# One-hots for two chunks from one two-operand comparison, in a four-layer graph network kernel

## What is computed

```python
x = layernorm(x + gat(x, ...))                  # layer 0
# layer 1: rows of a table summed by destination
h   = x @ W
out = segment_sum(h[src] * norm[:, None], dst, N)
x = layernorm(x + out)
# layer 2: twice, with edge weights
h   = x @ W1
out = segment_sum((dinv[row] * w * dinv[col])[:, None] * h[row], col, n) + b
x = layernorm(x + relu(...))                    # second time with W2
x = layernorm(x + layer3(x))                    # layer 3: same sums, the other direction
```

## Time and profile before

| | us |
|---|---|
| median of 3 runs (lowest, highest) | 3349.37 (3339.74, 3351.67) |
| the profiled execution: its own time | 3360.17 |
| its span, first to last instruction | 3358.4 |
| pass 1 (gathers) | 230.7 to 1413.3 |
| pass 2 (gathers) | 1430.7 to 2108.1 |
| pass 3 (gathers) | 2109.4 to 2794.2 |
| last layer, no gathers | from 2804 |

### The profile page before, as it was taken

The page is one execution under the profiler, slowest core; times in us unless marked ns, Lnnn a source line. Parts: engine busy times, 40 slices in busy tenths (PEclk is TensorE's granted clock), DMA queues, the critical chain, the costliest instruction groups (busy, mean ns, idle before and its releaser), DMA issues.

```text
span 3358.4 us, 58810 instructions
## 1 busy us (share of the span) xinstructions
PE 3159.1 (94%) x18605; PEld 2556.9 (76%) x18605; DVE 2313.6 (69%) x9060; ACT 1722.8 (51%) x4557; POOL 2046.4 (61%) x2015
## 2 busy tenths in 40 slices
PE   6789999999999999899999999799999998999999
PEld 5666777767767767678878888688888886888887
DVE  5657998998999889667777777466666664323323
ACT  3554767767767767534444444344444443232232
POOL 6627777777777777677777777577777772000000
PEclk9889999999999999999999999899999999999999
DMA  6256878778878778666666666676666666444443
GB/s 198 76 178 190 252 239 251 249 235 255 253 237 258 245 228 257 213 200 198 204 195 203 203 200 203 226 216 212 213 213 211 213 201 230 149 140 154 166 166 116
DMA packets 335272, 692.21 MB, mean 206 GB/s; under 512 B 63028, under 2 KB 180496, under 8 KB 334062
## 3 DMA queue, kind: packets, MB, share of 16 engines
q1 hardware_dynamic: 237134, 424.16, 37.4%
q0 software_dynamic: 95888, 262.38, 27.9%
q10 hardware_dynamic: 1936, 1.84, 0.2%
HBM read 497.33 MB, written 190.82 MB: 205 GB/s over the span
## 4 chain that ended last, share of the span: by engine, by line
PE 68%; DVE 12%; DMA 10%; POOL 4%; ACT 3%; issue 3%; SPq 0%; ACTq 0%; DVEq 0%
PE PS L1927 22%; PE PS L1999 15%; DMA G<-T,idx 7%; PE PS L1968 7%; PE PS L1970 6%; PE PS L1891 3%; POOL G L2062 2%; PE PS L1757 2%; PE PS L1867 2%; PE PS L1758 2%; DVE soh L1375 2%; PE PS L1858 2%; PE PS L1879 2%; PE PS L1908 1%; DVE M L1266 1%
## 5 line engine op out<-in xcount | busy, mean ns | idle before, releaser
L2062 POOL DMA_INDIRECT G<-T,idx x1890 | 1925.8, 1019 | 647.5 <-issue 275.4
L1927 PE MATMUL PS<-H,aw 128*128 128x256 f32 x4116 | 1052.0, 381 | 0.4 <-DMA aw<-AW 0.4
L1612 ACT ACTIVATE R<-G,wD 128x256 fp32r<-128x256 f32 x1008 | 508.8, 508 | 714.5 <-PE PS L1970 443.3
L1927 PEld LDWEIGHTS PS<-H,aw 128*128 128x128 f32 x4116 | 770.9, 191 | 110.5 <-DMA aw<-AW 0.8
L1275 DVE SCALAR_TENSOR_TENSOR R<-G,wD,R 128x256 fp32r<-128x256 f32 x1008 | 490.1, 486 | 389.4 <-ACT R L1612 385.2
L1968 PE MATMUL PS<-G,M 128*128 128x257 f32 x1764 | 572.5, 408 | 82.3 <-DMA G<-T,idx 32.5
L1970 PE MATMUL PS<-R,Mr 128*128 128x512 f32 x1008 | 583.6, 580 | 31.3 <-DVE R L1275 29.2
L1999 PE MATMUL PS<-HH,cr 128*128 128x512 f32 x2205 | 501.5, 389 | 0.3 <-DVE cr L1453 0.2
L1999 PEld LDWEIGHTS PS<-HH,cr 128*128 128x128 f32 x2205 | 413.3, 188 | 88.3 <-DVE cr L1453 2.6
L1655 ACT CAST atp<-PS 128x512 bf16<-128x512 f32 x588 | 336.5, 572 | 180.8 <-PE PS L1879 174.7
L1968 PEld LDWEIGHTS PS<-G,M 128*128 128x128 f32 x1764 | 297.9, 198 | 160.1 <-DVE M L1266 22.1
(11 more groups left out here) (231 smaller groups left out, 3908.5 us busy)
## 6 DMA issues: line engine op xcount, KB each, us to landing
aw<-AW SPq DMA_DIRECT2D x294, 448.0 KB
AT<-atp SPq DMA_DIRECT2D x539, 128.0 KB
br<-AT SPq DMA_DIRECT2D x77, 896.0 KB, 4.9
AW<-awp SPq DMA_DIRECT2D x264, 256.0 KB
G<-T,idx POOLq DMA_INDIRECT x1890
AT<-atf SPq DMA_DIRECT2D x49, 256.0 KB
T<-H SPq DMA_DIRECT2D x96, 128.0 KB
cr<-AT SPq DMA_DIRECT2D x7, 1024.0 KB, 4.8
```

The lines of the kernel that those rows point to most:

```text
L1612: e.activation(R[m % NR][:, 0:D], G[slot][:, 0:D], ACT.Copy, scale=wD[:, k // NC, k % NC:k % NC + 1]).then_inc(s_rw, 1)
L1927: ins = e.matmul(ps, aw[n_ % NAW][:, s_ % 7, :], H[:, s_, :], start=s_ == 0, stop=s_ == NBK - 1)
L2062: e.indirect_dma_start(G[slot][:, 0:D], None, TAB[p][0:N, :], bass.IndirectOffsetOnAxis(ap=idx[:, k // NC, k % NC:k % NC + 1], axis=0)).th ...
```

## The change

- `onehot` acts on even m only, and writes the one-hots of chunks m and m + 1 at once into a tile of 128 x 128 x 2: element (j, i) is 1 where `dlo` of chunk m + i is j. The two one-hots lie interleaved, element by element. It is a `tensor_tensor` whose two inputs are `iot2` (the ramp with each number twice, 256 columns) and two columns of `dlo`, repeated.
- NM is 3 tiles of two chunks; the pair m, m + 1 waits for the matmul of chunk m - 5.
- PE takes its stationary operand from the tile with a step of two elements (8 bytes). In pass 1 a matmul waits for the pair's instruction.
- `iot2` is written once, early, by a copy.

```diff
-NG, NM, NX = 7, 4, 4
+NG, NM, NX = 7, 3, 4
...
-        M = [tiles(onehots)(f"M{i}", [P, P]) for i in range(NM)]
+        M = [tiles(onehots)(f"M{i}", [P, P, 2]) for i in range(NM)]
         onehots.close()
-        Mr = [sb(f"Mr{i}", [P, P], F32R) for i in range(NM)]
+        Mr = [sb(f"Mr{i}", [P, P, 2], F32R) for i in range(NM)]
+        iot2 = sb("iot2", [P, P, 2])
...
+            done(e.tensor_copy(iot2[:, :, :], iot[:, :].unsqueeze(2).to_broadcast([P, P, 2])), "iot2")
...
             def onehot(p, k):
                 m = MOFF[p] + k
                 b, c = k // NC, k % NC
-                w.wait_ge(s_mm, m - NM + 1)
-                if p == 1:
-                    ins = e.tensor_scalar(M[m % NM][:, :], iot[:, :], dlo[:, b, c:c + 1], None, ALU.is_equal)
-                else:
-                    ins = e.tensor_scalar(Mr[m % NM][:, :], iot[:, :], dlo[:, b, c:c + 1], None, ALU.is_equal)
-                done(ins, ("M", m))
+                if m % 2 == 0:
+                    w.wait_ge(s_mm, m - 2 * NM + 2)
+                    done(e.tensor_tensor((M if p == 1 else Mr)[m // 2 % NM][:, :, :], iot2[:, :, :],
+                                         dlo[:, b, c:c + 2].unsqueeze(1).to_broadcast([P, P, 2]), ALU.is_equal), ("M", m))
...
-                    w.wait_ge(s_v, at["M", m] if p == 1 else at["low", m])
+                    w.wait_ge(s_v, at["M", m - m % 2] if p == 1 else at["low", m])
...
-                        e.matmul(ps, M[m % NM][:, :], G[slot][:, 0:D + 1], start=c == 0, stop=c == NC - 1).then_inc(s_mm, 1)
+                        e.matmul(ps, M[m // 2 % NM][:, :, m % 2], G[slot][:, 0:D + 1], start=c == 0, stop=c == NC - 1).then_inc(s_mm, 1)
                     else:
-                        e.matmul(ps, Mr[m % NM][:, :], R[m % NR][:, :], start=c == 0, stop=c == NC - 1).then_inc(s_mm, 1)
+                        e.matmul(ps, Mr[m // 2 % NM][:, :, m % 2], R[m % NR][:, :], start=c == 0, stop=c == NC - 1).then_inc(s_mm, 1)
...
-    nc = bacc.Bacc("TRN2", target_bir_lowering=False, num_devices=1)
+    nc = bacc.Bacc("TRN2", target_bir_lowering=False, num_devices=1, dynamic_dma_scratch_size=4096)
```

More of the change, by code:

```diff
@@ L1429, in aggregate @@
                     w.wait_ge(s_wn, 6)
+                after("iot2")
                 onehot(p, 0)
```

## The result

The changed kernel takes **3364.91 us** (median of 7 runs, 3356.97 to 3375.29) where the kernel before, timed beside it, takes 3347.86 (median of 7, 3339.74 to 3351.67). The ratio is 1.0057, 95% interval 1.0041 to 1.0073: slower by 14 to 24 us, 19 by the ratio, 17 by the medians. One warning on what follows: in two of the four later groups of runs the kernel before itself took 3838 and 3786 us, and those runs are compared only with the runs of before in their own group.

What follows compares the result with a forecast made beforehand. POOL's gathers were taken to bound passes 1 and 2, PE's dense units pass 3. Delays of 18.5 + 10.6 + 0 less 5.8 back gave +23.3 us on 3349.4: 3372.7 us, range 3338 to 3405 (8 in 10).

Steps and rivals of the forecast that it cites:

- POOL bounds passes 1 and 2: Gathers plus 0.305 us steps fill pass 1 (1173 of 1184 us) and pass 2 (679 of 679).
- The price of 42 ns: Gather delay per new two-input comparison, ends 0 and 90: 18.5 us in pass 1, 10.6 in pass 2.
- The counts of passes 2 and 3: Pass 2 taken as 504 gathers, 252 pairs; pass 3 as 505 gathers with 34 us to spare.
- What the removed one-hots cost POOL: Gathers starting beside old one-input one-hots, 0.02 us each: 5.8 us back, ends 0 and 12.
- By pass: Pass 1 longer by 12 to 20 us, pass 2 priced at 10.6, pass 3 unchanged.
- DVE's time at nothing: DVE relieved of 38 us over 945 pairs, hidden by POOL in passes 1 and 2 and PE in pass 3.
- Weights at a step at nothing: PE's weight loads at a step of 8 bytes were priced at 0 us.
- Loads over 200 ns: Sign set to prove the forecast wrong: PE's weight loads of L1970 or L1968 taking over 200 ns.
- The wait and the descriptor space at nothing: DVE's pair waiting for matmul m - 5, and the smaller gather descriptor space: 0 us each.
- The one-hots held POOL up: Rival, 12%: the old one-hots delayed gathers in passes 1 and 2, so the change is faster, 3315 us.
- Hardly delays: Rival, 25%: new comparisons delay gathers only 10 ns each, adding 7 us with 5.8 back: no change, 3350.5 us.
- Slow weights: Rival, 5%: 1008 weight loads in passes 2 and 3 each show 0.1 us, adding 100 us: 3473 us.

Runs made afterwards that it cites:

- scratch_only: The kernel before with only the smaller space for gather descriptors (4096): 3348.29 us, ratio 0.9990 to before.
- step_only: The changed kernel, but each one-hot written by its own one-input comparison into every second element of the shared tile: 3352.68 us, ratio 1.0000 to before.
- flat_tiles: The changed kernel with the pair's two one-hots one behind the other, so weights lie without a step: 3369.82 us, ratio 1.0059 to before.
- pass1_only: The changed kernel with the two-input comparison in pass 1 alone, one-input comparisons in passes 2 and 3: 3360.01 us, ratio 1.0028 to before.
- extra_two_again: The changed kernel plus 482 two-input comparisons in passes 1 and 2, into a tile nobody reads: 3431.29 us, ratio 1.0243 to before.
- extra_one_again: The changed kernel plus 482 one-input comparisons of the same output in passes 1 and 2, into an unread tile: 3390.80 us, ratio 1.0121 to before.

## Why the prediction came out as it did

The forecast was 3372.7 us, the measured median is 3364.9, inside the range of 3338 to 3405 (the forecast stood on 3349.4 for before, which the seven runs put at 3347.9); slower by over 0.5%, given 49%, is where the ratio of 1.0057 lies, though its interval reaches down across that bound.

- **POOL bounds passes 1 and 2: right.** In every kernel that was slower while before took some 3350 us, the gathers of the two passes are longer. Against the 1435.5 us of scratch_only and step_only they grew by 15 us in flat_tiles and 14 in pass1_only, whose medians lie 18 and 8 us above before, with DVE and PE less busy or as busy as before; in extra_two_again and extra_one_again they grew by 92 and 49 us, and the medians by 77 and 36. PE's wait for gathers rose as said.
- **The price of 42 ns: right on the mean, by luck in part.** The table gives 29.8 us over 441 + 261 = 702 new comparisons of passes 1 and 2: 42 ns. But it is 21.9 us over 441 in pass 1, 50 ns, and 7.9 over 261 in pass 2, 30 ns; one price for both passes was too low in one and too high in the other, and the two errors cancel. It is a price for these places only. Put right in front of another two-input comparison the same instruction costs 120; the end of 90 was too low for that, since it left out how joins close.
- **The counts of passes 2 and 3: a slip.** The window's edge was taken for the end of pass 2. It has 261 pairs, not 252, worth 0.4 us. POOL's bound there stands: 541.4 + 522 x 0.305 = 701 of 702.3 us. Pass 3 has 486 gathers, and before 479.8 us of them: 479.8 + 486 x 0.305 = 628 of 642.9 us. That leaves 15 us to spare, not 34, which still covers the 10.6 priced there.
- **"What the removed one-hots cost POOL", 5.8 us with ends 0 and 12: the term that was mis-sized.** The table puts it at 7.8 to 10.7 us, 9.2 on the mean. The prediction priced each at 0.02 us, with one place shown, where nothing was delayed, though a third of those gathers (52 of 152 in before) take 1 us or more: 23 are let in at the end of the one-hot itself and 27 at the end of a two-input instruction behind it. With 9.2 the sum is 29.5 - 9.2 = 20.3 us; with 5.8 it was 23.3. Both lie inside the interval of 14 to 24, so the times alone do not tell them apart.
- **A term that the prediction did not have.** Gathers that start outside the one-hots are held up some 5 us less with pairs than without (the account under the table). Why was not tested. It is of the size of what the sum is still too high by (20.3 against the measured 17 to 19) and somewhat larger.
- **By pass: half right.** Pass 1 was to grow by 12 to 20 us; pass1_only says 9.4, the profile pair 7.6, and three traces against three some 10. Pass 2 then brings 8 to 10 by the times and 6 by the traces, where 10.6 and a share of the 5.8 back were forecast. The profile pair shows nothing in pass 2, because before's profile had an unusually long one there. The mean gather was to grow by 15 to 25 ns in both passes, and grew less: from 1020 and 1022 ns (scratch_only, step_only) to 1034, 1033 and 1038 in pass 1, from 1027, 1023 and 1022 to 1036 and 1034 in pass 2. Pass 3 stayed, as said: its mean gather grew from 987 to 991 ns, and its length of 642.9 us not at all.
- **DVE's time at nothing: right.** 70 us less busy, 0 us gained.
- **Weights at a step at nothing: right in cost, wrong in the sign I set for it.** "Loads over 200 ns" was to prove it wrong. L1969 reads 204 ns on the mean, where L1968 read 198, and step_only, which has the longer loads, takes as long as before, so the sign came true and the cost did not. The Trainium skill (SBUF — State Buffer, the section "Door 1") says that two accesses to a 16-byte line are enough for full rate, which this step gives; the loads read 197 ns against 190, so nearly.
- **The wait and the descriptor space at nothing: right**, by step_only and scratch_only. That PE waits for the pair's instruction in pass 1 was not run by itself.
- **The rivals.** "The one-hots held POOL up" (3315) fell: without them the gathers are longer, not shorter. It held a grain of truth, the 9.2 us. "Hardly delays" (3350.5) lies below the interval, whose lower end is 1.0041 x 3347.9 = 3361.6. "Slow weights" (3473) fell with step_only and flat_tiles.
- **The rule of the Trainium skill** (SBUF — State Buffer, "Who interferes with whom") infers that `tensor_tensor` leaves descriptor generation alone. The prediction went by the rows against it, and flat_tiles against scratch_only bears that out: the same one-hots computed, the same descriptor space, gathers 15.5 us longer in two passes, and 21 us more time.

While the kernel before took about 3350 us, none of the kernels run was faster; scratch_only, at 0.9990, is no different from it. For `tensor_tensor` in pass 3 alone, which the slack there would hide, no run was made: DVE's saving is hidden there as well.

## What to carry to other kernels

When GpSimd's gathers set the pace, count VectorE's instructions with two SBUF inputs, and look at what follows each of them without a pause: merging two one-input instructions into a two-input one saved VectorE time here that nobody wanted, and took GpSimd time that everybody waited for. Price an instruction by the gathers that start inside it, over what a gather takes when undisturbed, and do it for the removed ones with the same care as for the added. And do not read half a per cent out of one pair of profiles: here the executions profiled by chance hid three quarters of it.

## What the runs showed that I had not expected

- **A join between two DVE instructions can stay shut, most often before a `tensor_tensor`.** In the places shown, a waiting gather got in where a `tensor_scalar` followed (1903.09), an L1275 (1897.21) or a pause (1612.71), but not where a `tensor_tensor` had begun about 0.08 us before the end of a two-input forerunner (1896.87, 1612.04, 1612.38). The count over the eight traces with before at some 3350 us bears that out as a tendency, not as a rule. It takes the gathers of passes 1 and 2 longer than 990 ns, and, of the ends of two-input instructions at least 150 ns after such a gather's start, what the next instruction was, where it had begun at least 40 ns before:

| next instruction | let in | passed by |
|---|---|---|
| `tensor_scalar`, one input | 2086 | 67 |
| `scalar_tensor_tensor`, two inputs | 393 | 11 |
| `tensor_tensor`, two inputs | 606 | 973 |
| none begun by then (a pause) | 314 | 1 |

  Behind a one-input forerunner a `tensor_tensor` shuts the join as well: 54 let in, 254 passed by. The place at 1347.71 is thus one of the fewer. What in the instruction makes the difference was not tested by itself.
- **The price rises steeply with crowding:** 42 ns for each of 702 comparisons, 120 for each of 482 more placed in front of them; 40 for the same number with one input.
- **4-byte weights at a step of 8 bytes** load in 197 ns against 190 at the median (step_only, flat_tiles), hidden here.
- **Paired one-hots are not slower everywhere.** Where before took 3838 and 3786 us and POOL did not bound pass 1, the four kernels with paired one-hots were 0.3 to 0.4% faster than before. That the bound is the reason is likely and not shown. What slows the chip at such times, and what the pairs save there, stays open.
